# Two graph transformer layers on one core: zeroing of the edge table paced by the mixing, graph attention's first blocks on an earlier wait, first chunk's sums on VectorE

## What is computed

```python
s = jnp.einsum('ehd,ehd->eh', q[src], k[dst]) / np.sqrt(D) + att_bias
m = jax.ops.segment_max(s, src, num_segments=n)
p = jnp.exp(s - m[src])
denom = jax.ops.segment_sum(p, src, num_segments=n)
alpha = p / jnp.where(denom[src] == 0, 1.0, denom[src])
agg = jax.ops.segment_sum(alpha[:, :, None] * v[dst], src, num_segments=n)
```

## Time and profile before

| | us |
|---|---|
| median of three executions | 2308.97 |
| lowest and highest | 2303.43, 2315.51 |
| the profiled execution | 2303.62 |
| its span, first to last instruction | 2301.9 |
| PE busy | 2084.8 (91%) |
| DVE busy | 1312.4 (57%) |
| POOL busy | 808.7 (35%) |
| DMA, share of 16 engines: from SP, from POOL | 24.0%, 5.9% |

### The profile page before, as it was taken

The page is one execution under the profiler, slowest core; times in us unless marked ns, Lnnn a source line. Parts: engine busy times, 40 slices in busy tenths (PEclk is TensorE's granted clock), DMA queues, the critical chain, the costliest instruction groups (busy, mean ns, idle before and its releaser), DMA issues.

```text
span 2301.9 us, 31846 instructions
## 1 busy us (share of the span) xinstructions
PE 2084.8 (91%) x11907; PEld 1271.3 (55%) x11907; DVE 1312.4 (57%) x3960; ACT 713.6 (31%) x1526; POOL 808.7 (35%) x558
## 2 busy tenths in 40 slices
PE   5999876898985999998999999999999999999977
PEld 3556544443332555555775456677777754455554
DVE  5655999567981776772224544442222234279997
ACT  4211122221001554442222355554211102135552
POOL 1336888887885766760000000000000000014443
PEclk9998887899998999999999999999999999999989
DMA  9994222223224988864000010002200005000000
GB/s 331 387 374 114 4 3 3 3 3 58 3 3 78 236 221 226 212 176 162 1 1 10 0 75 1 1 1 94 90 1 1 1 5 146 0 1 10 10 14 15
DMA packets 104811, 176.88 MB, mean 77 GB/s; under 512 B 64513, under 2 KB 66203, under 8 KB 94698
## 3 DMA queue, kind: packets, MB, share of 16 engines
q1 hardware_dynamic: 59585, 173.38, 24.0%
q0 software_dynamic: 45072, 1.46, 5.9%
HBM read 106.65 MB, written 68.15 MB: 76 GB/s over the span
## 4 chain that ended last, share of the span: by engine, by line
PE 48%; POOL 17%; DMA 13%; DVE 10%; issue 5%; ACT 4%; SPq 2%; DVEq 0%; PEldq 0%; ACTq 0%; POOLq 0%; PEld 0%
POOL edge_table L595 16%; PE banks L203 12%; DMA edge_table<-arena 8%; PE banks L2227 6%; PE banks L2269 6%; DMA arena<-edge_table 4%; PE banks L1576 3%; PE banks L2055 2%; PE banks L2043 2%; PE banks L2030 2%; PE banks L2653 2%; PE banks L1381 2%; PE banks L1401 2%; PE banks L2079 2%; DVE arena L1294 1%
## 5 line engine op out<-in xcount | busy, mean ns | idle before, releaser
L203 PE MATMUL banks<-arena 128*125 128x512 f32 x1200 | 557.3, 612 | 16.2 <-DVE arena L2873 14.4
L595 POOL DMA_INDIRECT edge_table<-arena x313 | 492.3, 1573 | 212.9 <-DMA edge_table<-arena 116.2
L203 PEld LDWEIGHTS banks<-arena 128*125 128x125 f32 x1200 | 222.7, 194 | 266.6 <-issue 248.1
L1294 DVE TENSOR_TENSOR arena<-banks,arena 125x1000 f32<-125x1000 f32 x100 | 194.3, 1963 | 110.3 <-DMA arena<-edge_table 56.0
L2680 POOL CAST arena<-arena 125x128 f32<-125x128 uint32 x10 | 2.9, 292 | 699.2 <-DVE arena L2816 699.2
L1327 POOL TENSOR_TENSOR arena<-arena 125x1000 f32<-125x1000 f32 x90 | 206.6, 2314 | 102.8 <-DVE arena L1294 97.0
L2175 DVE SCALAR_TENSOR_TENSOR arena<-banks,arena 125x512 f32<-125x512 f32 x80 | 60.1, 751 | 189.4 <-PE banks L2269 189.4
L2227 PEld LDWEIGHTS banks<-arena 128*128 128x128 f32 x1280 | 144.0, 192 | 6.7 <-issue 6.6
L1922 DVE CUSTOM_DVE_ANT_0 arena<-banks,arena 125x512 f32<-125x512 f32 (+8 forms) x144 | 73.0, 553 | 129.0 <-PE banks L2030 126.2
L2227 PE MATMUL banks<-arena 128*128 128x125 f32 x1280 | 146.4, 276 | 0.1
L2269 PE MATMUL banks<-arena 128*125 128x512 f32 x320 | 139.2, 593 | 0.0
(11 more groups left out here) (366 smaller groups left out, 3536.7 us busy)
## 6 DMA issues: line engine op xcount, KB each, us to landing
edge_table<-arena SPq DMA_DIRECT2D x23, 2304.0 KB, 24.9
arena<-edge_table SPq DMA_DIRECT2D x50, 984.4 KB
arena<-L_ffn_W SPq DMA_DIRECT2D x4, 2048.0 KB, 10.1
arena<-edge_table SPq DMA_DIRECT2D x50, 114.3 KB
adjacency<-arena SPq DMA_DIRECT2D x50, 109.4 KB
arena<-adjacency SPq DMA_DIRECT2D x10, 546.9 KB
edge_table<-arena POOLq DMA_INDIRECT x313
arena<-x SPq DMA_DIRECT2D x1, 2240.0 KB
```

Of the source, the lines that this page charges most:

```text
L203: last = nc.tensor.matmul(dst, xT[:, i, :], w[:, i, 0:n], start=(i == 0), stop=(i == k - 1))
L595: pool.indirect_dma_start(d["table"], bass.IndirectOffsetOnAxis(ap=cell[0:EP, c:c + 1].bitcast(U32), axis=0), vals[0:EP, c * ROW:(c + 1) * ...
L1294: nc.vector.tensor_tensor(weights_of(m).rearrange("p (s e n) -> p s e n", s=2, e=2), unit_scores(m).rearrange("p e (s n) -> p s e n", s=2) ...
```

## The change

- **Zeroing.** The 23 parts keep their size but are written in 12 lines of 384 floats per partition instead of 8 of 576; a tail replaces the rest. Two parts alone go ahead of Wq, Wk and Wv. The other 21 and the tail are issued one at a time: ten as the mixing's projections end, five along its attention, seven along its feed-forward part, each only when the one before has landed. The zeros lie elsewhere, so graph attention's weights load after the tenth of these.
- **What the scatters wait for.** At columns 0, 64, 160 and 240 POOL waits for as many parts as the largest cell of the columns up to the next of these marks needs; from column 240 on, for all. DVE works the counts out at the start.
- **First blocks.** DVE and PE find the last column that holds an edge with dst below 1000 (blocks 0 to 7 of the first chunk); SP waits for the columns up to it, and for column 160, ahead of the first blocks, and for all only ahead of block 8. In the first ten blocks the third buffer is memory where the dense product lay, so its store moves ahead of block 2. PE's wait for the table goes, and three unused products stay of seven.
- **Sums.** The 18 running sums of the first chunk go from POOL to DVE; POOL begins with the second chunk.

```diff
-        ZERO_LINE, ZERO_LINES = 576, 8
-        zeros = arena[:, BIG:BIG + ZERO_LINE]
+        ZERO_LINE, ZERO_LINES = 384, 12
...
-        EARLY = 8
+        KEY_TURNS = (0, 8, 20, 30)
+        KEY_MAXIMA = len(KEY_TURNS) - 1
...
+        zeros = marks.take(ZERO_LINE)
...
+        ZERO_ROWS = ZERO // ROW
         ZERO_PARTS = TABLE_ROWS * ROW // ZERO
-        ZERO_REST = (TABLE_ROWS * ROW - ZERO_PARTS * ZERO) // EP
-        REST_LINES = 9
-        assert EP * ZERO_REST + ZERO_PARTS * ZERO == TABLE_ROWS * ROW and ZERO_REST % REST_LINES == 0
+        TAIL_LINE = 328
+        TAIL = EP * ZERO_LINES * TAIL_LINE
...
         ZERO_FIRST = 2
-        FIRST_ROWS = ZERO_FIRST * ZERO // ROW
-        ZEROED_FIRST = 16 * (ZERO_FIRST + 1)
-        ZEROED_REST = 16 * (ZERO_PARTS - ZERO_FIRST) + 1
+        LATER = ZERO_PARTS + 1 - ZERO_FIRST
+        ZEROED_FIRST = 16 * ZERO_FIRST
+        ZEROED_REST = 16 * LATER + 1
...
-            sp.dma_start(flat[ZERO_PARTS * ZERO:TABLE_ROWS * ROW].rearrange("(p r a) -> p r a", p=EP, r=REST_LINES),
-                         zeros[:, 0:ZERO_REST // REST_LINES].unsqueeze(1)
-                         .to_broadcast([EP, REST_LINES, ZERO_REST // REST_LINES])).then_inc(s_table0, 16)
             for w, n in ((wq_m, "Wq"), (wk_m, "Wk"), (wv_m, "Wv")):
                 sp.dma_start(w.rearrange("p k n -> p (k n)"), d["L0_mix_" + n]).then_inc(s_wm, 16)
-            for n in range(ZERO_FIRST, ZERO_PARTS):
-                zero_part(sp, n, s_table1)
+
+        def zero_rest(sp):
+
+            pace = [(m_proj, 3 * n) for n in range(1, TILES + 1)]
+            pace += [(m_wo, n) for n in range(2, TILES + 1, 2)]
+            pace += [(m_f2, n) for n in (1, 2, 4, 5, 7, 8, 10)]
+            assert len(pace) == LATER
+            for i, (done, count) in enumerate(pace):
+                sp.wait_ge(done, count)
+                sp.wait_ge(s_table1, 16 * i + 1)
+                zero_part(sp, ZERO_FIRST + i, s_table1)
+                if i == TILES - 1:
+                    gnn_w_sp(sp)
...
-            nc.vector.tensor_reduce(hmax[0:EP, 0:1], key[0:EP, 0:EARLY * TC], AX_X, ALU.max)
...
+            for i in range(KEY_MAXIMA):
+                nc.vector.tensor_reduce(hmax[0:EP, i:i + 1], key[0:EP, KEY_TURNS[i] * TC:KEY_TURNS[i + 1] * TC], AX_X, ALU.max)
...
+            link(dve, nc.vector.tensor_scalar(parts, hmax[0:1, 24:24 + KEY_MAXIMA], 1.0 / ZERO_ROWS, 1.0 - ZERO_FIRST,
+                                              ALU.mult, ALU.add))
+            link(dve, nc.vector.tensor_scalar(whole, parts, 0.0, float(LATER), ALU.max, ALU.min))
+            nc.vector.tensor_scalar(zeroed_needed, whole, 16.0, 1.0, ALU.mult, ALU.add).then_inc(s_hstep, 1)
...
-            pool.wait_ge(s_table1, need)
 
             for c in range(USED):
-                if c == EARLY * TC:
-                    pool.wait_ge(s_table1, ZEROED_REST)
                 if c % TC == 0:
                     pool.wait_ge(s_group, c // TC + 1)
+                for i, n in enumerate(KEY_TURNS):
+                    if c == n * TC:
+                        pool.wait_ge(s_table1, need[i] if i < KEY_MAXIMA else ZEROED_REST)
...
+        SOON_TILES = 8
+        SOON_KEY = float(SOON_TILES * TP * NODES + 1)
+        ALL_EVEN, ALL_ODD = 16 * -(-USED // 2), 16 * (USED // 2)
+        needed_even, needed_odd = (pairs_needed[0:1, 2 + v:3 + v].bitcast(U32) for v in range(2))
+
+        def count_columns_dve(dve):
+            link(dve, nc.vector.scalar_tensor_tensor(out=away[0:EP, 0:USED], in0=key[0:EP, 0:USED], scalar=SOON_KEY,
+                                                     in1=pair_of[0:EP, 0:USED], op0=ALU.is_lt, op1=ALU.mult))
+            nc.vector.tensor_reduce(pairs_needed[0:EP, 0:1], away[0:EP, 0:USED], AX_X, ALU.max).then_inc(s_need, 1)
+
+        def turn_columns_pe(pe):
+            pe.wait_ge(s_need, 1)
+            nc.tensor.matmul(bank(7)[0:1, 256:256 + EP], pairs_needed[0:EP, 0:1], ident[0:EP, 0:EP],
+                             start=True, stop=True).then_inc(s_need, 1)
+
+        def needed_columns_dve(dve):
+            dve.wait_ge(s_need, 2)
+            link(dve, nc.vector.tensor_reduce(pairs_needed[0:1, 0:1], bank(7)[0:1, 256:256 + EP], AX_X, ALU.max))
+            link(dve, nc.vector.tensor_scalar(pairs_needed[0:1, 1:2], pairs_needed[0:1, 0:1], 16.0, 1.0, ALU.mult, ALU.max))
+            nc.vector.tensor_scalar(needed_even, pairs_needed[0:1, 1:2], float(ALL_EVEN), None, ALU.min).then_inc(s_need, 1)
+            nc.vector.tensor_scalar(needed_odd, pairs_needed[0:1, 1:2], float(ALL_ODD), None, ALU.min).then_inc(s_need, 1)
+
+        def soon_filled(sp):
+            sp.wait_ge(s_need, 4)
+            even = nc.sync.value_load(needed_even, min_val=1, max_val=ALL_EVEN)
+            odd = nc.sync.value_load(needed_odd, min_val=1, max_val=ALL_ODD)
+            sp.wait_ge(s_scat[0], even)
+            sp.wait_ge(s_scat[1], odd)
+            for v in range(2):
+                sp.wait_ge(s_scat[v], 16 * (CLEAR // 2))
...
         def gnn_w_sp(sp):
-            table_zeroed(sp)
...
+            table_zeroed(sp)
             sp.wait_ge(s_sum, TURNS)
...
+                if n == TURNS - 1:
+                    count_columns_dve(dve)
+                if n == TURNS:
+                    needed_columns_dve(dve)
...
+        aside = arena[:, BIG:BIG + CHUNK * ROW].rearrange("p (n w) -> p n w", w=ROW)
+        CLEAR = 160
+        assert 33792 + 2 * CHUNK * ROW <= 36864 + CLEAR * ROW
+        DVE_SUMS = PER - 2
...
+            return aside if i < TILES and i % RING == RING - 1 else ring[i % RING]
...
-            table_filled(sp)
+            soon_filled(sp)
...
+                if i == SOON_TILES:
+                    table_filled(sp)
+                spread(sp, edge_block(i)[0:TP, :, :], table[tok(b), sources(c), :], s_tab[i % RING])
 
             for i in range(RING):
+                if i == RING - 1:
+                    sp.wait_ge(f_step, 5)
+                    sp.dma_start(d["wgd"], wgd_out.rearrange("p k n -> p (k n)")).then_inc(s_fold, 16)
+                    sp.dma_start(d["l1_bias"], bias_out[0:1, :]).then_inc(s_fold, 16)
+                    sp.wait_ge(s_fold, 32)
                 load_block(i)
...
-                if i == TILES:
-                    sp.wait_ge(f_step, 5)
-                    sp.dma_start(d["wgd"], wgd_out.rearrange("p k n -> p (k n)")).then_inc(s_fold, 16)
-                    sp.dma_start(d["l1_bias"], bias_out[0:1, :]).then_inc(s_fold, 16)
                 if i == 2 * TILES:
-                    sp.wait_ge(s_fold, 32)
...
+                if 2 <= m - 1 < 2 + DVE_SUMS:
+                    sum_weights(nc.vector, dve, m - 1)
...
+        def sum_weights(ops, eng, m):
+            c, b, h = place(m)
+            eng.wait_ge(a_p, m + 1)
+            if b == 1:
+                eng.wait_ge(a_pv, m - 1)
+            else:
+                eng.wait_ge(a_sum, m - 2 * (c + 1) - 1)
+            total_p = psum_g[c % 2][0:TP, 2 * h:2 * h + 2, :].rearrange("p s n -> p (s n)")
+            ops.tensor_tensor(total_p, total_p, weights_of(m), ALU.add).then_inc(a_sum, 1)
+
         def att_pool(pool):
-            for m in range(UNITS):
-                c, b, h = place(m)
-                if b == 0:
-                    continue
-                pool.wait_ge(a_p, m + 1)
-                if b == 1:
-                    pool.wait_ge(a_pv, m - 1)
-                else:
-                    pool.wait_ge(a_sum, m - 2 * (c + 1) - 1)
-                total_p = psum_g[c % 2][0:TP, 2 * h:2 * h + 2, :].rearrange("p s n -> p (s n)")
-                nc.gpsimd.tensor_tensor(total_p, total_p, weights_of(m), ALU.add).then_inc(a_sum, 1)
+            pool.wait_ge(a_sum, DVE_SUMS)
+            for m in range(2 + DVE_SUMS, UNITS):
+                if place(m)[1]:
+                    sum_weights(nc.gpsimd, pool, m)
...
-            table_filled(pe)
             pe.wait_ge(f_step, 5)
-            for n in range(7):
+            for n in range(3):
```

More of the change, by code:

```diff
@@ L251, in gps_two_layers @@
         total = edge.take(TC * ROW)
+        pair_of = edge.take(EC // 2).bitcast(BF16)
+        pairs_needed = edge.take(4)
         early = Space(2 * SLOT, 3 * SLOT)
@@ L256, in gps_two_layers @@
         ident16 = early.take(EP // 2).bitcast(F16)
+        MAXIMA = KEY_MAXIMA + HEADS
         hmax = early.take(48)
+        zeroed_needed = hmax[0:1, 44:44 + KEY_MAXIMA].bitcast(U32)
+        pair_i = early.take(EC + 2)
         rest = arena[:, 2 * SLOT:2 * SLOT + EC * ROW]
@@ L308, in const_pool @@
                            channel_multiplier=1)
+            nc.gpsimd.iota(pair_i[0:EP, :].bitcast(I32), pattern=[[1, EC // 2 + 1], [0, 2]], base=1, channel_multiplier=0)
             nc.gpsimd.memset(parts3[:, 0:3 * ROW], 0.0)
@@ L547, in parts_pool @@
         def parts_pool(pool):
-            pool.wait_ge(s_hstep, 5)
-            need = nc.gpsimd.value_load(hmax[0:1, 33:34].bitcast(U32), min_val=1, max_val=ZEROED_REST)
+            pool.wait_ge(s_hstep, 6)
```

(6 more changed lines are left out.)

35 lines of the change are left out of this document (19 added, 16 removed).

## The result

| | before | after |
|---|---|---|
| median of 12 executions, us | 2307.89 | 2320.08 |
| lowest and highest | 2303.43, 2315.51 | 2314.13, 2323.93 |
| the profiled execution | 2303.62 | 2316.72 |
| its span | 2301.9 | 2314.9 |

The ratio is 1.0052 with the interval 1.0042 to 1.0062: half a per cent slower, where 2287 and faster were predicted, and outside the range. Between the profiled executions the difference is 13.1 us.

A forecast was written before the change was run, and what follows sets the result against it. POOL's scatters were taken to bound the kernel by delaying attention; terms of -28.3, -5.0, +1.2, +3.1, +5.1 and +4.7 us summed to -19.2, giving 2284.4 for a profiled execution and 2287 as median, range 2271 to about 2307.

The forecast's parts named there:

- pacing: Zeroing parts beside POOL's scatters: 21 parts at 3.6 us each, last column issued at 736, 9 us later than before.
- the lone burst of the earlier trace: Three 1 MB loads at 550 beside the scatters: a loss of 5.65 us, by bytes 4.2 for a zeroing part.
- Block 8: SP's wait for all columns in attention's first chunk: +4.7 us, with loads and store delaying the last columns some 14 us.
- scatters dearer, the table late at block 8: Rival at SP's wait ahead of block 8: 5.65 us a part gives 2328; chance 0.08 for slower, 0.06 for no change.
- the first rival: Scatters beside zeroing parts cheaper to disturb, 2.4 us a part: 2279.7, about 2282 as a median; chance 0.14.
- Start: The mixing's first matmul, waiting for Wv: -5.0 us, as the zeroing's rest no longer goes ahead of Wv.
- POOL's waits: POOL's new waits for zeroing parts at marked columns: cost nothing by themselves.
- Start of attention: DVE's first attention product: -28.3 us, starting at 704.7 when the dense product ends instead of waiting for all scatters.
- Block 2: Attention's third block load, behind the store of the dense product: +3.1 us, unit 4 at 719.6.
- Sums on DVE: The first chunk's running sums, moved from POOL: +5.1 us, 1.13 us a sum and 3.04 a unit.
- The third rival: Attention's first chunk: DVE's sums cost 1.91 us each, as much as a product; 2297, chance 0.08.
- The early wait does nothing: Rival at the first blocks: the earlier wait fails, so attention starts after the scatters at 746; 2318, chance 0.04.

The follow-up runs named there:

- e3: The changed kernel with SP waiting for all columns ahead of the first block, as before the change; 2342.88 us against 2302.44 for the kernel before.
- e8: The kernel before with Wq, Wk and Wv behind two zeroing parts and the rest of the zeroing last; 2297.06 us against 2301.0, ratio 0.9982.
- e12: The changed kernel with parts in four pieces, each issued when the one before landed, without waits for the mixing's tiles; 2277.05 us against 2305.27, ratio 0.9861.
- e7: The changed kernel with each paced part in four pieces, each issued when the one before has landed; 2283.57 us against 2301.0 for the kernel before.

## Why the prediction was wrong

**The step that failed: pacing.** "Every part costs the scatters something wherever it is put" was right, and 21 parts met columns, as counted. But I took 3.6 us a part from the steady row, "which is zeroing itself", and not the lone burst of the earlier trace rows. Measured: 96 us from column 8 to 128. The part at 184.46 and the three weight loads right behind it cost 8.9 us together (186.35 to 200.75 for three columns), so the loads alone are worth some 4.4, an estimate from the price of the other parts. That leaves about 91 for 21 parts, 4.3 each. That is what the lone burst gave by bytes (4.2); against 1.85 us a column instead of 1.91 single parts cost 3.7 to 6.6, 4.6 in the mean. The heading "about nothing for the time in which scatters end" fell too, though the sum under it had 9 us. It took no account of how many parts pass for free when they are all in one queue: before, nearly eight were issued by column 8 and 5.8 of them had moved; paced, 1.3 had. Column 279 came at 688.1 instead of 674: 21 x 0.7 = 15 us for the price, 4.4 for the weight loads (which I had not charged at 185), less 5 because column 8 came at 69.8 and not at 74.9.

**Block 8.** The mechanism was as predicted (SP's wait, 10.8 us from the last column's issue to the first product; measured 11.7), but the term was undersized by half: the loads and the store cost the last 33 columns 27 us (e3 against the kernel after), not 14, a little over my upper bound of 25. With the late column 279 that gives 776.9 for the last column instead of 750, and unit 20 at 801.6 instead of 773: 28.6 us missed, of which 26.9 are the last column's.

**Which rival it was.** The second, "scatters dearer, the table late at block 8", at its place and beyond the point I gave for it (the last column near 769). I gave it 0.08. Its price was smaller than the 5.65 I had tried, and the loads made up the rest. What should have told: the steady 3.5 us are for parts back to back, and the change makes every part a lone one; the only lone burst in the trace was the better row.

**The rule of the Trainium skill** (DMA: Bandwidth & Descriptors, Queues, rings and completion order), that a DMA engine takes turns between its queues packet by packet, I had read as a scatter waiting only for packets; that gave 2.4 a part and the first rival. The runs don't bear this reading out for whole parts: lines of 384 and 576 lose 96 and 99 us, and the column caught at 213.71 had its first packets 4.4 us after the part's. My other reading, that a caught pair lands only with the burst's end, goes a little too far: that column's packets were through at 220.50, the part's at 222.06.

**What was right.**
- *Start*: 9.0 us instead of 5.0, near the upper bound of 9.4; 0.73 us of the wait for Wv are left. e8 shows that alone it is worth 0.18%.
- *POOL's waits*: nothing. The marked columns 64, 160 and 240 are issued at 223.89, 455.87 and 615.57 with 1.08, 0.32 and 0.37 us idle ahead of them.
- *Start of attention*: first product at 702.0 (704.7), but by luck. The dense product, which was to end the wait, was done at 697.1; the block ended it, because the columns up to 281 were 14 us late. In e12, where they are early, the dense product does end it (698.6). e3 shows that without the earlier wait the first product would start at 764.0.
- *Block 2*: unit 4 at 717.4 (719.6), in part by luck too: the store held the block's load from 697.14 to 708.35, 11.2 us where 6.5 were taken, but it started with a dense product that was earlier than forecast.
- *Sums on DVE*: 1.11 us from a sum's start to the next product's (1.13; its row says 1.18) and 2.97 a unit (3.04). The rule of the Trainium skill on the shared port pair (SBUF — State Buffer, SBUF: two separate sides) would have cost 1 us a column by my estimate. The trace doesn't agree: beside the sums of 745 to 753 columns pass at 1.85 us, apart from one of 2.24. The third rival, sums at the product's price, is out.
- *The early wait does nothing*: out, by e3.

**Open.** Beyond unit 99 the changed kernels' profiled executions lose some 3 us more (2.7 after, 3.1 with e7, 3.2 with e12) in stages that none of them touches. 1.6 us of it arise between 1578 and 1624 in each of them, and in e8 as well, which is the kernel before in these stages; so this much belongs to the profiled execution of before and not to the change. The rest is open. Why a piece of 0.59 MB takes 3.5 us in its chain wasn't split into its parts. Three columns in flight instead of two, which a burst might hold up less, weren't tried, nor were pieces under 0.59 MB.

## What to carry to other kernels

Where a chain of small transfers, each waiting for the last, sets the end, the bulk transfers beside it cost by the length of each burst, not by their bytes: cut them and wait between the pieces before you think of moving them. A bulk transfer is free only where the chain isn't running yet, so pacing it by other work's progress can move it from the free place into the paid one. And price a transfer that will stand alone by a row in which one stands alone.

## What the hardware showed beyond that

The size of the effect of cutting was not expected: 96, 73 and 32 us lost for the same bytes in pieces of 2.36, 1.18 and 0.59 MB, while whole parts in one queue cost 71. And a single issue can be long. The loads of the earlier trace rows, three of 1 MB, go out at 536.6 to 537.4 in the kernel after, and POOL's timeline reads:

```profile
541.72 1.54 POOL L618 DMA_INDIRECT edge_table<-arena  x1 [2.71 <-DMA edge_table<-arena]
545.54 1.54 POOL L618 DMA_INDIRECT edge_table<-arena  x1 [2.29 <-DMA edge_table<-arena]
547.39 6.01 POOL L618 DMA_INDIRECT edge_table<-arena  x1 [0.30 <-DMA edge_table<-arena]
```

Columns 200 to 212 took 31.3 us here and 22.8 before. The loads cost 4.4 of that (537.47 to 547.39 for three columns), less than the 5.65 of the earlier trace rows. Another 4.5 are one column's issue that held POOL for 6.01 us instead of 1.54, when the loads' packets had ended (546.25). What made it long isn't known, and no experiment was made on it.
